# Top-2 experts of three row chunks in four, run on rows sorted by expert through DRAM, instead of all eight experts on every row

## The reference, cut to what matters

```python
x = x + ffn0(attention(x, ...))                  # relu(a @ w1 + b1) @ w2 + b2
h = gelu(x @ fc1.T + fc1_b)                      # 256 -> 1024
c = concat(h @ fc2.T + fc2_b, h @ experts_w[index[b]].T + experts_b[index[b]])   # 1024 -> 256
probs = softmax(c @ router_w.T)                  # 8 experts
topk_vals, topk_idx = top_k(probs, 2)
topk_w = topk_vals / (topk_vals.sum(-1) + 1e-6)
out = x + sum_k (c @ expert_weights[topk_idx[k]] + probs[topk_idx[k]]) * topk_w[k]
```

## Time and profile before

| | |
|---|---|
| median of 3 runs | 569.72 us (569.52 to 570.09) |
| profiled execution, its time / its span | 570.82 us / 568.4 us |
| TensorE, VectorE, ScalarE, GpSimd busy | 92%, 72%, 40%, 15% of the span |
| mean granted TensorE clock | 0.98 |
| DMA | 15.37 MB, 27 GB/s over the span |

### The profile page before, as it was taken

The page is one execution under the profiler, slowest core; times in us unless marked ns, Lnnn a source line. Parts: engine busy times, 40 slices in busy tenths (PEclk is TensorE's granted clock), DMA queues, the critical chain, the costliest instruction groups (busy, mean ns, idle before and its releaser), DMA issues.

```text
span 568.4 us, 7403 instructions
## 1 busy us (share of the span) xinstructions
PE 521.5 (92%) x2649; PEld 360.3 (63%) x2649; DVE 408.6 (72%) x788; ACT 225.7 (40%) x381; POOL 84.2 (15%) x94
## 2 busy tenths in 40 slices
PE   3897888999899999889969999999999999999896
PEld 1454445454454445436748887888878888788775
DVE  4887879878887777845867598483884839847295
ACT  4204476667665656764526240042400415003100
POOL 3002544315133120300141000010000100000000
PEclk9999699999999999999999999999999999999999
DMA  7200011101010000000451000100001000010000
GB/s 250 57 2 0 1 37 38 37 2 38 1 39 1 1 0 2 1 1 0 114 146 38 1 1 20 46 10 0 2 18 47 11 2 0 20 46 2 9 12 31
DMA packets 11756, 15.37 MB, mean 27 GB/s; under 512 B 5954, under 2 KB 8258, under 8 KB 11714
## 3 DMA queue, kind: packets, MB, share of 16 engines
q1 hardware_dynamic: 11714, 14.83, 8.5%
HBM read 12.73 MB, written 2.10 MB: 26 GB/s over the span
## 4 chain that ended last, share of the span: by engine, by line
PE 39%; DVE 6%; POOL 2%; issue 1%; DMA 1%; ACT 1%; SPq 0%; DVEq 0%; POOLq 0%
PE psG L1546 4%; PE psG L1545 4%; PE psG L1544 4%; PE psM L1544 3%; PE psM L1545 3%; PE psM L1546 3%; PE psS L1544 3%; PE psS L1545 3%; PE psS L1546 3%; PE psO L1544 3%; PE psO L1546 3%; PE psO L1545 3%; DVE hT_lo L1694 1%; DVE hT_hi L1692 1%; DMA staged<-ew_dram 1%
## 5 line engine op out<-in xcount | busy, mean ns | idle before, releaser
L737 DVE TENSOR_REDUCE few_Qa<-psG 128x2 fp32r<-128x512 f32 x116 | 74.7, 686 | 28.5 <-PE psG L506 28.4
L657 ACT ACTIVATE Pr<-psS 128x512 f32<-128x512 f32 x128 | 71.4, 599 | 28.5 <-PE psS L528 19.5
L744 DVE SCALAR_TENSOR_TENSOR Pr<-Pr,few_W 128x1024 f32<-128x1024 f32 x48 | 72.8, 1520 | 10.2 <-ACT Pr L657 10.1
L524 PE MATMUL psS<-few_QAT,few_KP 128*128 128x512 f32 x128 | 52.9, 457 | 10.5 <-ACT Pr L657 9.8
L504 PE MATMUL psG<-few_KG,QG 128*128 128x512 f32 x116 | 53.0, 515 | 2.9 <-DVE few_Qa L737 2.9
L1655 ACT ACTIVATE V<-psS,cols 128x512 f32<-128x512 f32 x16 | 11.0, 690 | 103.3 <-PE psS L1546 102.6
L1694 DVE TENSOR_TENSOR hT_lo<-V,hT_hi 128x512 fp32r<-128x512 f32 x64 | 46.5, 726 | 2.2
L506 PE MATMUL psG<-Mneg,few_identb 128*128 128x512 bf16 x116 | 46.8, 403 | 0.0
L524 PEld LDWEIGHTS psS<-few_QAT,few_KP 128*128 128x128 f32 x128 | 22.3, 188 | 38.2 <-issue 30.7
L1692 DVE CAST hT_hi<-V 128x512 fp32r<-128x512 f32 x64 | 34.2, 535 | 12.7 <-ACT V L1655 6.2
L540 PE MATMUL psO<-Pr,few_VA 128*17 128x512 f32 x256 | 33.5, 598 | 0.0
(11 more groups left out here) (251 smaller groups left out, 1194.7 us busy)
## 6 DMA issues: line engine op xcount, KB each, us to landing
Pr<-xT_dram SPq DMA_DIRECT2D x2, 1024.0 KB, 8.6
staged<-w_dram SPq DMA_DIRECT2D x4, 512.0 KB, 3.7
x1T<-xT_dram SPq DMA_DIRECT2D x4, 512.0 KB, 4.2
staged<-ew_dram SPq DMA_DIRECT2D x4, 512.0 KB, 4.0
out_dram<-y SPq DMA_DIRECT2D x16, 128.0 KB, 1.7
staged<-fc_dram SPq DMA_DIRECT2D x2, 512.0 KB, 3.8
Pr<-wqkv_dram SPq DMA_DIRECT2D x1, 768.0 KB, 4.9
staged<-fc2a_dram SPq DMA_DIRECT2D x1, 512.0 KB, 3.4
```

Of the source, the lines that this page charges most:

```text
L524: mm = nc.tensor.matmul(psS[:, f, :], self.KP[:, u % 2, j, r * P:r * P + P], self.QAT[:, u % 2, j // 2, q], start=True, stop=not logged)
L657: nc.scalar.activation(Pr[:, i % JOBS, 512 * f:512 * f + 512], psS[:, f, :], ACT.Exp, scale=SCALE).then_inc(self.s["s_exp"], 1)
L737: nc.vector.tensor_reduce(self.Qa[:, f % SLOTS, st, 2 * p:2 * p + 2, 48], self.guard_bank(i)[0][:, p, :].rearrange("p (h t) -> p h t", h=2 ...
L744: nc.vector.scalar_tensor_tensor(pr, pr, FMAX, self.W[:, r, :], ALU.min, ALU.mult).then_inc(self.s["s_prob"], 1)
```

## The change

Chunks 0 to 2 (`SORTED = 3`) no longer run their experts one chunk later. In place of the 20 jobs, chunk c has for chunk c - 1:

- "rows" (2 jobs, behind h's first): c's fp32 output in V is transposed to rows (8 transposes) and copied to crow by VectorE. GpSimd scatters every row twice, by indirect DMA, to the DRAM tensor `room`: 8 experts with 1536 rows each. `room` is filled with zeros before, by eight DMAs in SP's order between the second and the third weight piece.
- "rank" (1 job, before h's last two): two small bf16 matmuls count, per row and expert, the rows before it; VectorE turns this to the place of each row. With chunk 2's, it also works out which expert and which rows each of 31 blocks of 128 rows has.
- "base" (4 jobs, before y): the transposes of x1T and the addition of pw, kept in attT's columns.

After gelu of chunk 3, before its c stage, come 31 blocks. For each, SP loads 128 rows from `room` at a row number read from a register ("turned": 2 transposes; ScalarE makes hi, VectorE lo), then "sorted": 6 matmuls of 256 columns with the expert's weights at an address from a register; ScalarE copies the result, SP stores it to `made`. TensorE and SP read eight registers at a time. When all blocks are stored, GpSimd gathers by 24 indirect DMAs. Chunk 3's experts run at the end as before, and after each 128 rows stand three "mix" jobs, each two VectorE passes that add the two gathered results, scaled, to the kept row, and a store.

```diff
+SORTED = 3
+ROOM = SORTED * QC
+BLOCKS = 2 * ROOM // P + NE - 1
+BLOCK_AHEAD, ROW_RING, SPLIT_RING, OUT_RING, REGS = 3, 8, 4, 4, 8
...
             for c in range(CHUNKS + 1):
+                in_order = 0 < c <= SORTED
                 if c < CHUNKS:
-                    yield from jobs_of("h", c, range(KW // 2), "act")
+                    yield from jobs_of("h", c, range(1), "act")
+                    if in_order:
+                        yield from jobs_of("rows", c - 1, range(TT // 2), "dve")
+                    yield from jobs_of("h", c, range(1, KW // 2), "act")
                 if c:
                     yield from jobs_of("router", c - 1, range(1), "dve")
                 if c < CHUNKS:
-                    yield from jobs_of("h", c, range(KW // 2, KW), "act")
-                if c:
+                    yield from jobs_of("h", c, range(KW // 2, KW - 2), "act")
+                    if in_order:
+                        yield from jobs_of("rank", c - 1, range(1), "dve")
+                    yield from jobs_of("h", c, range(KW - 2, KW), "act")
+                if in_order:
+                    yield from jobs_of("base", c - 1, range(TT), "dve")
+                elif c == CHUNKS:
+                    for t in range(TT):
+                        yield from jobs_of("experts", c - 1, range(5 * t, 5 * t + 5), "dve")
+                        for i in range(SORTED * t, SORTED * (t + 1)):
+                            yield "mix", i // TT, i, "", 0
+                elif c:
                     yield from jobs_of("experts", c - 1, range(behind), "dve")
                 if c < CHUNKS:
                     yield from jobs_of("y", c, range(KD), "dve")
...
                     yield from jobs_of("gelu", c, range(KW), "act")
...
+                    if c == SORTED:
+                        for i in range(BLOCKS + BLOCK_AHEAD):
+                            if i < BLOCKS:
+                                yield from jobs_of("turned", c, range(i, i + 1), "dve")
+                            if i >= BLOCK_AHEAD:
+                                yield from jobs_of("sorted", c, range(i - BLOCK_AHEAD, i - BLOCK_AHEAD + 1), "act")
...
+                if stage == "turned":
+                    pe.wait_ge(rows_sem[i % ROW_RING], 16 * (i // ROW_RING + 1))
+                    for k in range(KD):
+                        mm = nc.tensor.transpose(ps[:, k * P:k * P + P], block_rows[:, i % ROW_RING, k * P:k * P + P], ident)
+                if stage == "sorted":
+                    weights("ew")
+                    if i % REGS == 0:
+                        pe.wait_ge(d["blocks_known"], 1)
+                        now = pe_regs[0:min(REGS, BLOCKS - i)]
+                        pe.load(now, expert_at[0:1, i:i + len(now)])
+                        block_expert = [pe.snap(r, min_val=0, max_val=(NE - 1) * D) for r in now]
+                    pe.wait_ge(d["v_out"], number["turned", c, i] + 1)
+                    of = bass.ds(block_expert[i % REGS], D)
+                    for k in range(KD):
+                        mm = mm3(ps[:, 0:D], parts(blockT, ALL, i % SPLIT_RING, k, ALL), parts(ew[k], ALL, of),
+                                 k == 0, k == KD - 1)
...
+                if stage == "sorted":
+                    if i >= OUT_RING:
+                        act.wait_ge(out_sem[i % OUT_RING], 16 * (i // OUT_RING))
+                    nc.scalar.copy(block_out[:, i % OUT_RING, :], ps[:, 0:D]).then_inc(d["a_out"], 1)
...
+                    for t in range(TT):
+                        for k in range(2):
+                            nc.gpsimd.indirect_dma_start(
+                                room[:, :], bass.IndirectOffsetOnAxis(ap=place_in[:, c, k, t:t + 1], axis=0),
+                                crow[:, t, :], None).then_inc(d["scattered"], 16)
...
+            pool.wait_ge(d["placed_out"], 1)
+            for i in range(OUT_RING):
+                pool.wait_ge(out_sem[i], 16 * len(range(i, BLOCKS, OUT_RING)))
+            for i in range(SORTED * TT):
+                for k in range(2):
+                    nc.gpsimd.indirect_dma_start(
+                        returned(2 * i + k), None, made[:, :],
+                        bass.IndirectOffsetOnAxis(ap=place_out[:, i // TT, k, i % TT:i % TT + 1], axis=0)).then_inc(back_sem[i // SORTED], 16)
...
+                if stage == "mix":
+                    dve.wait_ge(back_sem[i // SORTED], 32 * SORTED)
+                    o = kept(c, i % TT)
+                    for k in range(2):
+                        settle()
+                        ins = nc.vector.scalar_tensor_tensor(o, returned(2 * i + k), share[:, c, k, i % TT:i % TT + 1], o,
+                                                             ALU.mult, ALU.add)
...
+        def clear_rows(sp):
+            for i in range(NE):
+                sp.dma_start(room[i * ROOM:(i + 1) * ROOM, :].rearrange("(p r) e -> p (r e)", p=P),
+                             io["zeros"]).then_inc(d["cleared_rows"], 16)
...
+            def block_rows_in(i):
...
+                if i >= ROW_RING:
+                    sp.wait_ge(d["v_full"], number["turned", SORTED, i - ROW_RING] + 1)
+                sp.dma_start(block_rows[:, i % ROW_RING, :], room[bass.ds(first_rows[i % REGS], P), :]).then_inc(
+                    rows_sem[i % ROW_RING], 16)
...
+                if stage == "turned":
+                    if i == 0:
+                        sp.wait_ge(d["blocks_known"], 1)
+                        sp.wait_ge(d["scattered"], 16 * 2 * TT * SORTED)
+                        sp.wait_ge(d["v_full"], number["y", SORTED, KD - 1] + 1)
+                        for j in range(BLOCK_AHEAD):
+                            block_rows_in(j)
+                    if i + BLOCK_AHEAD < BLOCKS:
+                        block_rows_in(i + BLOCK_AHEAD)
+                if stage == "sorted":
+                    sp.wait_ge(d["a_out"], n + 1)
+                    sp.dma_start(made[i * P:i * P + P, :], block_out[:, i % OUT_RING, :]).then_inc(out_sem[i % OUT_RING], 16)
```

More of the change, by code:

```diff
@@ L1399, in bass_adaln_ffn @@
         WcB = Split("WcB", [B, KW, P])
-        ew = Split("ew", [KD, NE * D])
+        ew = [Split(f"ew{k}", [NE * D]) for k in range(KD)]
         WcA = Split("WcA", [KW, P])
@@ L1418, in bass_adaln_ffn @@
+        held = sb("held", [P, SORTED * TT_ + 1, NE], F32)
+        place = sb("place", [P, SORTED, 2, TT_], F32)
+        place_in = sb("place_in", [P, SORTED, 2, TT_], U32)
+        place_out = sb("place_out", [P, SORTED, 2, TT_], U32)
+        share = sb("share", [P, SORTED, 2, TT_], F32)
         if nc.sbuf_base < attention_end:
             sb("gap", [P, (attention_end - nc.sbuf_base + 3) // 4], F32)
[L1420 to L1422 removed]
@@ new lines, in bass_adaln_ffn, with kept, returned @@
+        staged = sb("staged", [P, 2, 1024], F32)
+        def kept(c, t):
+            a = c * QC + t % 2 * D
+            return attT[:, t // 2, a:a + D]
+        def returned(j):
+            n = back.shape[1]
+            return back[:, j, :] if j < n else staged[:, (j - n) // 4, (j - n) % 4 * D:((j - n) % 4 + 1) * D]
+        tables = [attT[:, k, SORTED * QC:(SORTED + 1) * QC] for k in range(KD)]
+        past = tables[0][:, 0:BLOCKS * NE].rearrange("p (s e) -> p s e", e=NE)
+        scratch = tables[0][:, 256:512]
@@ new lines, in bass_adaln_ffn, with table @@
+        at_ = iter(range(0, QC, 32))
+        def table(n):
+            a = next(at_)
+            for _ in range((n - 1) // 32):
+                next(at_)
+            return tables[1][:, a:a + n]
+        rows_of, blocks_of, blocks_before, blocks_to = table(NE), table(NE), table(NE), table(NE)
+        expert_of, before_of, first_row, left, moved = table(BLOCKS), table(BLOCKS), table(BLOCKS), table(BLOCKS), table(NE)
+        over = table(NE * (ROOM // P)).rearrange("p (e j) -> p e j", e=NE)
@@ L1425, in flat @@
+        expert_at = table(32).bitcast(I32)
+        row_at = table(32).bitcast(I32)
         def flat(w, n0, n):
@@ L1540, in bass_adaln_ffn, with read_last, turned_last @@
         number = {(stage, c, i): n for stage, c, i, e, n in jobs}
+        def read_last(c):
+            return number["router", c, 0] if c < SORTED else number["experts", c, TT * 5 - 1]
+        def turned_last(c):
+            return number["base", c, TT - 1] if c < SORTED else number["experts", c, TT * 5 - 5]
         def mm3(ps, w, a, start, stop):
@@ L1662, in dense_act @@
                     split_hi(act, late_at(stage, c, i))
-        split_of_act = [split_no[stage, c, i] for stage, c, i, e, n in jobs if e == "act"]
+        split_of_act = []
+        for stage, c, i, e, n in jobs:
+            if e == "act":
+                split_of_act.append(split_of_act[-1] if stage == "sorted" else split_no[stage, c, i])
         def attention_lo(pool, c):
@@ L1881, in _ @@
             setup_tensor(pe)
+            pe_regs.extend(pe.alloc_register(f"block_expert{j}") for j in range(REGS))
             def work(att):
```

240 lines of the change are left out of this document (214 added, 26 removed).

## The result

The changed kernel took **610.99 us** (median of 4 runs, 608.37 to 612.18) against 569.62 (568.10 to 570.09) for the kernel before: ratio 1.0725, 95% interval 1.0683 to 1.0767, slower by 41 us. The forecast was 593 (571 to 622). In three later comparisons, on three chips, the same program took 591.8, 594.6 and 590.6, and the kernel before 569.4 to 569.7 each time. So there are two results to explain: some 22 us that every comparison shows (21 to 25), and 16 to 20 more that only the first one has. Chips 5, 10 and 4 ran the later three; the chip of the first is not on record.

What follows compares the result with a forecast made beforehand. The prediction took TensorE's pace to bound the chunks before the change. Chunks -31.9, sorted stage +45 and tail +10.3 sum to +23.4; 570.8 + 23.4 - 1.1 = 593 us, slower, range 571 to 622.

Steps and rivals of the forecast that it cites:

- rivals 2 and 3: 2: sorted stage runs at 1.2 GHz, 612 us, chance 0.15; 3: gathers come late, 607 us, chance 0.15.
- Chunks, -31.9: Chunks 1 to 3 without the experts' matmuls: gains of 12.3, 12.3 and 7.3 us, between -28 and -40.
- a stop of 5.2: Before y in a chunk: TensorE stands 5.2 us, from 409.4 to 414.6, until VectorE's base0 eviction.
- gelu waits 2.12 (2.2): Between y and gelu: TensorE waits 2.2 us for x_lo instead of 5.44 of expert jobs, gain 3.2.
- The table: Chunk 3's block table on VectorE, 15 dependent steps in front of h6: 5 us.
- the clock, 1.5 us per chunk: At y's start, matmul time lost to a lower clock after the stop: 1.5 us per chunk, bounds 0 and 3.
- Sorted stage, +45: Between gelu and c of chunk 3: 31 blocks at 1.3 us plus start and register loads, +45 us (31 to 68).
- 2.8 was forecast for four: Sorted stage: four loads of eight registers on TensorE and SP, 0.7 us taken for each, 2.8 in sum.
- Tail, +10.3: At the end, VectorE gets 24 more passes after its 36, all at 0.52 us: +10.3 us (6 to 13).
- 9.1 (router, as from 534.98 to 544.12): In the tail, chunk 3's router up to the first experts pass takes 9.1 us, as in the kernel before.
- TensorE as the bound: Rival 1, whole kernel: TensorE stays the bound and the result is faster, 549 us, chance 0.10.
- Clearing: Rival 4: clearing holds the third weight piece, 614 us, or 655 if clearing takes 141 us; chance 0.06.

Runs made afterwards that it cites:

- Fourth comparison: The changed kernel unaltered, measured a fourth time against the kernel before: 590.6 us, ratio 1.039.
- first run: The changed kernel in its first comparison with the kernel before: 610.99 us, ratio 1.0725.
- run 8: On top of run 6, SyncE issues the sorted stage's row loads seven blocks ahead instead of three: 564.1 us, ratio 0.991.
- Runs 4, 5, 10 and 11: 4: changed kernel with base ahead of h4 to h7, rank behind h7, 573.2 us; 5, 10, 11: changed kernel unaltered, 591.8, 594.6, 590.6 us.
- run 6: Changed kernel with base early, plus ao jobs between y and gelu and block tables behind y0's split: 571.3 us, ratio 1.004.
- runs 8 and 9: 9: on top of run 8, chunk 3's two c jobs put between the blocks: 557.1 us, ratio 0.979.

## Why the prediction was right and wrong

The sum, +23.4 us and 593, is what three of four comparisons measured (590.6 to 594.6); the one it was made for came to 611. That 611 is still within 571 to 622 is luck: the upper end came from rivals 2 and 3, neither of which happened, and the chain that did grow stood in no term and no rival.

- **Chunks, -31.9.** Fourth comparison -32.7, first run -27.0. y starts 5.1 us behind the base transposes that it follows (a stop of 5.2 was forecast), and 1.6 of that lie already in front of base3, which needed the rank job's bank too; that link was not in my chain. gelu waits 2.12 (2.2). The table costs 5 us in chunk 3 (7.86 against 2.92). What was mis-sized is **the clock, 1.5 us per chunk, 4.5 in all**: about 6 in the later profile and 11 in the first, up to 4.7 in one chunk, because the stop of 2.12 in front of gelu could cost clock as well. My bound of 3 was too low, and the row it came from the earlier trace rows is one draw of something that varies.
- **Sorted stage, +45.** 43.6 and 44.5. TensorE's block is 0.93 us (transposes and six matmuls 0.12 apart), so 14.8 of the 43.6 us are not its own pace. The first run's trace has 9.8 of them as waits: 4.8 for row loads, 4.3 for VectorE's blockT_lo and 0.7 for a register load (2.8 was forecast for four; 1.4 in the fourth comparison). The loads were only three ahead, behind SyncE's waits, as said: run 8 shows it, and that it was worth 8.8 us.
- **Tail, +10.3.** +10.0 and +8.9 for the 24 passes. The 36 passes before took 20.9 us, 0.58 each and not 0.52; the 60 took 29.8 to 30.9, 0.50 to 0.51, so the gaps between them were filled and the two errors cancel. A gather takes 0.95 + 0.30 us on GpSimd against the assumed 1.3, all hidden.
- **The step that failed in the first run** is the "9.1 (router, as from 534.98 to 544.12)" inside the tail. I carried VectorE's chain of tiny dependent instructions over unchanged, though 24 new DMAs now lay beside it. It took 15.4 us more. Runs 4, 5, 10 and 11 show that such company alone doesn't do it; the first run's trace puts the gaps down to the instruction before, to "issue" and to "remote", which names no cause. The profile shows no loading of instructions during the longest gaps. Whether it is that chip, where the program's DRAM tensors lay, or something else is open.
- **Rivals.** TensorE as the bound: no, periods of 59. The sorted stage at 1.2 GHz: no, its granted clock was 1.00 in the first run and 0.96 in the fourth comparison. Late gathers: no, 1.25 us each; against the 3.1 us that the Trainium skill gives ("SBUF — State Buffer", SBUF: two separate sides) the longest of 24 beside VectorE's casts took 1.17, so nothing like it was met here. Clearing: no. The eight DMAs ran at 324 GB/s and were through by about 61 us, the third weight piece was issued at 73.1 and cast at 102.7, as in the earlier trace rows; I had charged them with 178 GB/s.

## What to carry to other kernels

When matmuls are taken away, look at what they stood in front of: here the experts had covered VectorE's splits, and putting base's evictions in front of four splits, and rank behind them, was worth 18 us. In a ring of transfers ask who issues the next load and what that engine waits for first; the depth of the loop was three although the buffers were eight. Compare two profiles from where their code begins to differ: 4.2 of the 7.7 us between runs 8 and 9 lay ahead of it. And repeat a comparison on another chip before a difference of 20 us is explained from one trace.

## What the runs showed of the hardware that I had not expected

- The same program's time differed by 16 to 20 us (3%) between the first comparison and the others while the medians of the kernel before stayed within 0.4 us; 15.4 us of it lie in one chain of small dependent VectorE steps whose starts were up to 4.6 us apart instead of about 0.25.
- After equal stops of 2.92 us TensorE ran at 1.2 GHz for over 5.29 us in one execution and over 2.73 in another, and after a stop of 2.12 us came 3.4 us at half clock or none. Periods of identical code came to 61.6, 59.0 and, in another order, 54.2 and 52.6 us.
- An indirect DMA of 128 rows of 1 KB holds GpSimd for 0.95 us, with 0.30 to the next, as a gather or a scatter (median 0.96 of the 48 in the first run, at most 1.22; the longest of all runs took 1.48, in run 6); GpSimd issued plain loads of the same size one every 0.53 us.
